# Softmax reciprocals of a four-tile head group spread, copied and divided once per group instead of once per unit

## The reference, cut to what matters

```
q = (x @ Wq).reshape(B, T, H, Dh)   # k, v alike
scores = jnp.einsum('bthd,bshd->bhts', q, k)
mask = jnp.tril(jnp.ones((T, T), dtype=scores.dtype))
scores = scores * mask
attn = jax.nn.softmax(scores / T ** 0.5, axis=-1)
out = jnp.einsum('bhts,bshd->bthd', attn, v).reshape(B, T, H * Dh)
return out @ Wo
```

## Time and profile before

| | |
|---|---|
| median of 3 runs | 1541.69 us (1541.46 to 1542.38) |
| the profiled execution | 1539.09 us, its span 1537.1 us |
| PE busy | 1443.9 us, 94% of the span |
| DVE, ACT, POOL busy | 1001.8, 731.4, 360.3 us |
| granted PE clock, mean | 0.984 |

### The profile page before, as it was taken

The page is one execution under the profiler, slowest core; times in us unless marked ns, Lnnn a source line. Parts: engine busy times, 40 slices in busy tenths (PEclk is TensorE's granted clock), DMA queues, the critical chain, the costliest instruction groups (busy, mean ns, idle before and its releaser), DMA issues.

```text
span 1537.1 us, 28299 instructions
## 1 busy us (share of the span) xinstructions
PE 1443.9 (94%) x8896; PEld 726.5 (47%) x8896; DVE 1001.8 (65%) x2126; ACT 731.4 (48%) x1684; POOL 360.3 (23%) x667
## 2 busy tenths in 40 slices
PE   6888989998899878799999999999999999999999
PEld 3465456555644644334444444444444444444444
DVE  7585668557746868778666566566666666666533
ACT  5795269338815854434433433433533533533522
POOL 0042014003300775462121121121121121121100
PEclk9999999999999999899999999999999999999999
DMA  7642422152243230101010000010010010000011
GB/s 243 153 147 91 111 90 75 64 148 70 85 123 101 79 113 16 43 16 32 16 32 16 17 31 16 16 32 17 17 32 16 17 31 16 16 32 1 1 55 55
DMA packets 68379, 87.67 MB, mean 57 GB/s; under 512 B 5760, under 2 KB 53120, under 8 KB 67840
## 3 DMA queue, kind: packets, MB, share of 16 engines
q1 hardware_dynamic: 68224, 85.74, 18.3%
HBM read 62.92 MB, written 22.81 MB: 56 GB/s over the span
## 4 chain that ended last, share of the span: by engine, by line
PE 63%; issue 18%; DVE 6%; ACT 5%; POOL 4%; SPq 2%; DMA 2%; ACTq 0%; POOLq 0%; DVEq 0%
PE bank L769 20%; PE bank L771 20%; PE bank L770 20%; ACT prob L1136 2%; PE bank L848 1%; PE bank L829 1%; POOL nmx L647 1%; POOL G L624 1%; SPq L450 1%; DVE xn L386 1%; DVE c L1617 1%; ACT prob_t L1152 1%; POOL pk L640 1%; POOL w_full L587 1%; DMA pk_in<-L_ffn_down_W_packed_dram 1%
## 5 line engine op out<-in xcount | busy, mean ns | idle before, releaser
L769 PE MATMUL bank<-xs,G 128*128 128x512 f16 x896 | 342.1, 382 | 14.9 <-POOL G L624 13.5
L770 PE MATMUL bank<-xs,G 128*128 128x512 f16 x896 | 341.8, 382 | 0.0
L771 PE MATMUL bank<-xs,G 128*128 128x512 f16 x896 | 341.6, 381 | 0.0
L1603 DVE TENSOR_TENSOR c<-bank,c 128x512 f32<-128x512 f32 x128 | 88.2, 689 | 199.1 <-PE bank L771 198.9
L1223 ACT COPY c<-bank 128x512 f32<-128x512 f32 x192 | 111.4, 580 | 213.7 <-PE bank L771 208.6
L769 PE MATMUL bank<-Wd,hid 128*128 128x512 f16 x512 | 194.6, 380 | 3.5 <-DVE X L1657 3.4
L770 PE MATMUL bank<-Wd,hid 128*128 128x512 f16 x512 | 194.6, 380 | 0.0
L771 PE MATMUL bank<-Wd,hid 128*128 128x512 f16 x512 | 194.6, 380 | 0.0
L632 POOL TENSOR_TENSOR c<-c,m 128x512 f32<-128x512 f32 x64 | 82.2, 1284 | 384.9 <-ACT c L1223 384.9
L1657 DVE SCALAR_TENSOR_TENSOR X<-bank,col,X 128x512 f32<-128x512 f32 x128 | 95.7, 750 | 102.7 <-PE bank L771 102.6
L1474 DVE CUSTOM_DVE_ANT_0 bank<-bank,mask,col 128x128 f32<-128x128 f32 (+3 forms) x256 | 138.9, 548 | 35.6 <-PE bank L818 31.4
(11 more groups left out here) (177 smaller groups left out, 2359.9 us busy)
## 6 DMA issues: line engine op xcount, KB each, us to landing
stack<-qk_dram SPq DMA_DIRECT2D x128, 128.0 KB, 3.3
sc_in<-scale_t SPq DMA_DIRECT2D x32, 384.0 KB
qk_dram<-qk SPq DMA_DIRECT2D x32, 256.0 KB, 2.3
packed_t<-pk_t SPq DMA_DIRECT2D x32, 192.0 KB, 1.9
pk_in<-packed_t SPq DMA_DIRECT2D x32, 192.0 KB
X<-in_x_dram SPq DMA_DIRECT2D x4, 1024.0 KB, 7.2
pk_in<-L_ffn_gate_W_packed_dram SPq DMA_DIRECT2D x16, 256.0 KB, 2.6
pk_in<-n_L_ffn_up_W_packed_dram SPq DMA_DIRECT2D x16, 256.0 KB, 2.9
```

The source lines that it names most:

```text
L769: pe.matmul(o, lhs(0), rhs(0), start=first, stop=False, skip_group_check=onto)
L770: pe.matmul(o, lhs(0), rhs(1), start=False, stop=False, skip_group_check=onto)
L771: return pe.matmul(o, lhs(1), rhs(0), start=False, stop=stop, skip_group_check=onto)
L1603: nc.vector.tensor_tensor(dst[:], bank[at][:], dst[:], ALU.add).then_inc(comb, 1)
```

## The change

The spreads of four units are done as one block of 16 matmuls into one whole bank, copied by ACT in one 512-wide copy and used by one 512-wide division. `r_col` keeps the columns of a whole group, the four units' values lie side by side in bank 6, and `o_done` and `rden_out` count groups. The block stands on PE in the next group's first unit behind the turn of head 2; ACT's copy at (second unit, head 2), behind that head's exponential and a turned copy; the division at (third unit, head 0), where before the division of a group's last unit stood. The copy goes into the space of `o_t`'s last group. The slots are renumbered, 76 in place of 88.

```
-        r_col = sb("r_col", [P, 2, 4], F32)
-        r_den = sb("r_den", [P, 2, P], F32)
+        r_col = sb("r_col", [P, 2, TT, 4], F32)
+        r_den = o_t[:].bitcast(F32)[:, :, HG - 1, :]
...
-            return h + 2 * (max(0, h - 2) // 16) + max(0, h // 4 - 1)
+            return h + 2 * (max(0, h - 2) // 16) + max(0, h - 3) // 16
...
-        def recip_slot(u):
-            return turn_slot(4 * u + 7) + 1 if u < UNITS - 1 else pack_slot(HG - 1, 1) + 1
+        def recip_slot(hg):
+            return turn_slot(16 * hg + 18) + 1 if hg < HG - 1 else pack_slot(HG - 1, 1) + 1
...
-        AT_RECIP, AT_DIVIDE = 9, 12
+        AT_RECIP, AT_DIVIDE = (1, 2), (2, 0)
...
-                if u >= 1:
-                    pe.wait_ge(o_done, n * UNITS + u)
+                if i == 0 and hg > 0:
+                    pe.wait_ge(o_done, n * HG + hg)
                 blocks = wide[i] // P
-                at = P * (u % 2)
+                at = P * i
...
+            def recips(n, hg):
+
+                slot = recip_slot(hg)
                 pe.wait_ge(*turn_read(n, slot - 3))
+                pe.wait_ge(rcol_done, n * UNITS + 4 * hg + 4)
+                for i in range(TT):
+                    for j in range(4):
+                        mm = pe.matmul(turn_bank(slot)[32 * j:32 * j + 32, P * i:P * i + P], r_col[:, hg % 2, i, j:j + 1].to_broadcast([P, DH]), ident[:],
+                                       start=True, stop=True)
...
                         turn(n, u, j)
+                        if j == 2 and u > 0 and u % TT == 0:
+                            recips(n, u // TT - 1)
                         if j == 3 and u > 0:
-                            recips(n, u - 1)
                             values(n, u - 1)
...
+            def recip_out(n, hg):
+                act.wait_ge(r_full, n * HG + hg + 1)
+                if hg > 0:
+                    act.wait_ge(o_done, n * HG + hg)
+                else:
+                    act.wait_ge(xf_stored, n * 16 + 16)
+                nc.scalar.copy(r_den, turn_bank(recip_slot(hg))[:].rearrange("p (a t) -> p a t", a=2)).then_inc(rden_out, 1)
...
-                        h = 4 * u + j - AT_RECIP
-                        if h >= 0 and h % 4 == 0:
-                            recip_out(n, h // 4)
+                        if u > TT and (u % TT, j) == AT_RECIP:
+                            recip_out(n, u // TT - 1)
...
+                dve.wait_ge(rden_out, n * HG + hg + 1)
+                dve.wait_ge(av_done, n * UNITS + TT * hg + TT)
+                nc.vector.scalar_tensor_tensor(o_sum[:].rearrange("p (a t) -> p a t", a=2), bank[6][:].rearrange("p (a t) -> p a t", a=2), QS, r_den, ALU.mult, ALU.mult).then_inc(o_done, 1)
```

More of the change, by code:

```diff
@@ L272, in turn_read @@
         def turn_read(n, slot):
+            for hg in range(HG):
+                if slot == recip_slot(hg):
+                    return rden_out, n * HG + hg + 1
             for u in range(UNITS):
-                if slot == recip_slot(u):
-                    return rden_out, n * UNITS + u + 1
                 for j in range(4):
@@ L1097, in body @@
                 repack(n, HG - 1)
-                recips(n, UNITS - 1)
+                recips(n, HG - 1)
                 if not last:
@@ L1152, in turned @@
                 nc.scalar.copy(prob_t[:, u % 2, j, 0:wide[i]], turn_bank(turn_slot(4 * u + j))[:, 0:wide[i]]).then_inc(pt_act, 1)
[L1154 to L1158, removed]
+            def recip_out(n, hg):
[5 more added lines that the diff above has]
+                nc.scalar.copy(r_den, turn_bank(recip_slot(hg))[:].rearrange("p (a t) -> p a t", a=2)).then_inc(rden_out, 1)
             def out_head(n, hg):
-                act.wait_ge(o_done, n * UNITS + 4 * hg + 4)
+                act.wait_ge(o_done, n * HG + hg + 1)
                 if hg == 0:
@@ L1375, in body @@
                             repacked(n, u // TT - 1)
-                        h = 4 * u + j - AT_RECIP
-                        if h >= 0 and h % 4 == 0:
-                            recip_out(n, h // 4)
+                        if u > TT and (u % TT, j) == AT_RECIP:
+                            recip_out(n, u // TT - 1)
                 turned(n, UNITS - 1, 2)
-                for u in range((ROWS - 1 - AT_RECIP) // 4 + 1, UNITS - 1):
-                    recip_out(n, u)
                 repacked(n, HG - 1)
-                recip_out(n, UNITS - 1)
+                recip_out(n, HG - 1)
                 if not last:
@@ L1501, in reciprocals, with divide @@
                     sums = den
[L1502 to L1507, removed]
+                nc.vector.reciprocal(r_col[:, u // TT % 2, u % TT, :], sums[:, u % 2, :]).then_inc(rcol_done, 1)
+            def divide(n, hg):
+                if hg > 0:
                     dve.wait_ge(o_hi, n * HG + hg)
                     dve.wait_ge(o_lo, n * HG + hg)
[L1510 to L1513, removed]
+                dve.wait_ge(rden_out, n * HG + hg + 1)
+                dve.wait_ge(av_done, n * UNITS + TT * hg + TT)
+                nc.vector.scalar_tensor_tensor(o_sum[:].rearrange("p (a t) -> p a t", a=2), bank[6][:].rearrange("p (a t) -> p a t", a=2), QS, r_den, ALU.mult, ALU.mult).then_inc(o_done, 1)
             def out_tail(n, hg):
@@ L1818, in body @@
                             reciprocals(n, u - 1)
-                        h = 4 * u + j - AT_DIVIDE
-                        if h >= 0 and h % 4 == 0:
-                            divide(n, h // 4)
+                        if u > TT and (u % TT, j) == AT_DIVIDE:
+                            divide(n, u // TT - 1)
                         if j == 0 and u % TT == 1 and u > TT:
@@ L1833, in body @@
                 turned(n, UNITS - 1)
-                for u in range((ROWS - 1 - AT_DIVIDE) // 4 + 1, UNITS - 1):
-                    divide(n, u)
                 repacked(n, HG - 1)
```

9 lines of the change are left out of this document (2 added, 7 removed).

## The result

The changed kernel takes **1547.26 us** (median of 6 runs, 1544.47 to 1549.56) where the kernel before, on the same chip, takes 1541.38 (1539.46 to 1542.38, 6 runs): a ratio of **1.0046, 95% interval 1.0031 to 1.0060**, slower by 7 us by this ratio and by 5.9 by the medians. In a second comparison the ratio was 1.0033 (1.0023 to 1.0043), 5 us. The profiled execution took 1549.56 us.

The account below looks back on a forecast made before the run. ACT was taken as the fullest engine, with PE setting its time at group boundaries. Sequences 1 and 2 (3.2), sequence 0 (0.6) and sequence 3 (0.3) gave +4.1 us on 1541.69: 1545.8; 8-in-10 range 1538 to 1549.5.

Parts of the forecast that it names:

- ACT's idle time: Sign: ACT idle ahead of a boundary's turned copy near 1.5 us, from 0.38; forecast wrong if under 0.8.
- the group window: Sign: one head group's window in the attention loop near 16.0 us where it was 15.15.
- TensorE's chain at a boundary: Between head groups, PE's work from the end of `pk_t`'s copy to the next unit's first turn: 1.63 to 2.47 us, +0.84.
- The exposed copy: At a boundary, ACT's 512-wide copy behind the copy that waits for the turn is paid in full: +0.46 us.
- the second turn: The next unit's second turn on PE waits for the bank the large copy frees: +0.10 us, bounds 0 and 0.2.
- What comes back: After each boundary two 0.14 copies are gone on ACT, before the next a 0.24 spread: 0.52 us back.
- DVE's stall: DVE's 0.98 us stall for POOL's tail at the first tile's division goes; 0.3 us back in the second group.
- The end of a sequence: Last spread and PE's wait for division go (1.32 us), twelve more spreads precede the next input's turn (0.72): net −0.60.
- Merging saves ACT about 0.1 us per group: Per group, four 128-wide ACT copies hold 0.56 us, one 512-wide 0.46; the skill page would give 0.43 saved.
- Sequence 0, +0.6: Same loss as other sequences, but ACT's waits on POOL after the first boundary take up 1.0 us: +0.6 us.
- Sequence 3, +0.3: POOL's weight work sets the pace and a 2.71 us wait hangs on a load: +0.3 us, bounds −0.5 and +2.5.
- a rival of 0.07: PE's new idle time at boundaries may lower the granted clock to 1.2 GHz, time near 1553 us; chance 0.07.

Follow-up runs that it names:

- The block twice over: Changed kernel with each block of 16 spread matmuls done two times, same result: 1559.85 us, ratio 1.0123 to the kernel before.
- the wide block alone: Kernel before with a group's last four spreads done four times over (16 matmuls), copies and divisions still small: 1549.22 us, ratio 1.0040.
- The copy one head sooner: Changed kernel with ACT's 512-wide copy moved to second unit, head 1: 1540.03 us, ratio 1.0003 to the kernel before.
- the kernels with the block off the chain: Changed kernel, spreads moved behind second unit's head 1 turn (copy, division, cast one head later): 1541.87 us, 1.0005; or behind its head 0 turn: 1543.80 us, 1.0010.
- the filled sequence 3: Changed kernel with 8 extra matmuls at heads 0 and 1 of three units in four, sequence 3 only: 1549.83 us, ratio 1.0048.

## Why the prediction was right, and what was off

The forecast was 1545.8 us, slower by 4.1; measured were 1547.26 and 1547.43 us, slower by 5.1 to 7.1 (0.33 to 0.46% of 1542). The mechanism is the one that was forecast; one of its sizes was off by more than its bounds allowed in one profile. By the profiles' means the sums of all four sequences were too low, by 0.8, 0.4, 0.5 and 1.8 us (7.7 in all for 4.1); that the total comes as near as it does is in part luck, since the timed runs give less than the profiles.

Of the signs, ACT's idle time is 1.34, 1.07 and 1.27 us where I had said near 1.5, and the group window 16.15 for 16.0; the waits named came and went as forecast.


- **TensorE's chain at a boundary, +0.84.** From the turned copy of (4,0) to that of (5,0) passed 3.77 us before (229.72 to 233.49) and pass 4.64 (231.41 to 236.05): +0.87. The block twice over (+0.86 per boundary) and the wide block alone (+0.64 for 0.72) show that it is this block.
- **The exposed copy, +0.46, and the second turn, +0.10.** The copy holds ACT 0.48; behind it the turned copy of (5,1) starts 0.24 after the start of `e_zero`'s row (237.26), which holds ACT 0.09: 0.15 late. The copy one head sooner takes 0.64 of this back.
- **What comes back, -0.52.** 0.87 + 0.48 + 0.15 = 1.50 us, and the part that no stall disturbed grew by 16.16 - 15.14 = 1.02: 0.48 came back.
- **DVE's stall, -0.3.** The stall is gone, but brought 0.2: the second of the two middle parts grew by 0.82 where the first grew by 1.02. The four parts of sequence 1 (+0.56, +1.03, +0.82, -0.40, means of the profiles) give +2.01 us where I had 1.60: the first part was forecast 0.10 too low (-0.38 + 0.84), the middle ones 0.39 (2 x 0.88 - 0.3).
- **The end of a sequence.** Forecast for the last part 0.46 + 0.10 - 0.28 - 0.60 = -0.32, measured -0.40.
- **Merging saves ACT about 0.1 us per group, not the durations.** The group of the large copies, beside which the earlier trace rows stands:

```profile
L1164 ACT COPY o_t<-bank 128x512 f32<-128x512 f32 x16 | 9.4, 591 | 2.4 <-PE bank L859 2.4
```

By durations that is 18.7 - 9.4 = 9.3 us less on ACT; its busy time over the kernel fell from 731.4 to 730.2, by 1.2 us, and 16 x 0.1 is 1.6. The Trainium skill (page "VectorE: DVE Perf Modes", section "The TRN2 errata — SBUF-src ops pay a fixed extra latency per instruction") gives a ScalarE instruction from PSUM 172 cycles plus one per element, the fixed part each time. As an estimate from this page, the kernels with the block off the chain should have gained 16 x 0.43, some 7 us. They took 1.0005 and 1.0010 of the time before, with waits of 0.23 and 0.67 us at the copy. The duration of a row agrees with the page (0.59 us, the estimate from the page 0.57), the time that it holds the engine does not.
- **Sequence 0, +0.6.** Measured +1.4 by the means (65.71 against 64.29). ACT's waits on POOL took up less of the delay than the 1.0 us that I had given them; the part behind the first boundary was 16.49 and 16.34 before and 17.01, 17.29 and 16.15 after.
- **Sequence 3, +0.3: the step that failed by size.** The profiled run lost 4.82 us there, beyond my bound of 2.5. Over the profiles the means are 77.18 and 75.07, +2.1, within the bound; three profiles from 74.98 to 79.20 against two of 74.38 and 75.76 don't fix this number well. I had reasoned with POOL's pace and held the clock for a rival of 0.07 that hits the boundaries of sequences 0 to 2. It hit none of those: TensorE's waits of 0.37 and 0.95 us there leave the clock at 1.00. (Sequences 1 and 2 begin at the low level in both kernels. In sequence 1 it lasts until about 220.4 and 219.4 us before and until 220.8, 223.0 and 221.0 in the three profiles of the changed kernel, whose first parts of 18.90, 19.40 and 19.26 us go with how long after their start that is.) It hit sequence 3, at one or two boundaries of each profile, where a boundary now has 2.5 us of TensorE work on ACT's path instead of 1.6 and so loses more to each low stretch. That last point is argued from the two lengths of one boundary, not tried by itself, and the rows give it little: between its two profiles the kernel before lost 1.4 us at the third boundary (idle time 1.83 for 0.40, the part 18.36 for 17.00), hardly less than the 1.56 of the changed kernel (I had put up to 1.8). They differ more in how often: the clock was low at the third boundary in one of two profiles before and in all three after. The load ahead of the last group, which I had seen as a wait of 2.71, moves the sequence as well (POOL's wait for it is 0.41 to 2.03 us in the five profiles), so how much of the +2.1 is the clock stays open. The page "TensorE: Matmul & The Clock Gate" of the Trainium skill, section "What's actually happening", has the throttled clock as the default that activity releases; the filled sequence 3, without a low stretch, agrees.
- **The rest.** The sequences' means give 1.42 + 2.02 + 2.14 + 2.11 = 7.7 us, and the spans' means 1545.6 - 1536.8 = 8.8; about 1 us lies between the sequences, which I did not resolve. The timed runs give less, 5.1 to 7.1; both profiled executions of the kernel before (1539.09 and 1538.43) lie below its medians, so the profiles show too large a difference.

## What to carry to other kernels

Merging small steps pays only by the time that they hold their engine, read from start to next start, not by their durations; and it turns work that was spread out into one piece that must stand somewhere. Look for the wait that engines already share (here the one behind `pk_t`), and keep the merged piece off the chain between it and its waiter, with the copy that follows ahead of the waiting instruction rather than behind it. Where one stage of a kernel has TensorE mostly waiting, profile it more than once before costing anything in it: a boundary there was 2.94 or 4.50 us long, and a wait for a load 0.41 or 1.60 us, in the same kernel.

## What the runs showed of the hardware that was not expected

- An ACT copy from a bank overlaps with the instruction behind it so far that four 128-wide ones (0.14 us each to the next start) cost hardly more than one 512-wide (0.48), though their durations are 0.27 and 0.59 us.
- In sequence 3 the granted clock falls to half, mostly for about 3 us at a time, in windows that change with the execution (from 518, 554 and 572 us on, from 500 and 554, from 500, 533 and 554 in the three profiles of the changed kernel). One and the same boundary is 2.94 us long at one level and 4.50 at the other. Eight more matmuls at each of 22 places, otherwise useless, kept the clock up throughout that sequence in the one profile, and left no gain.
